# Expert stage of a routed graph layer: the order in which ScalarE and VectorE prepare weights, tokens and results

## The reference, cut to what matters

```
gates = sigmoid(xt @ expert_sel.T);  top 4 experts of each token
scores = relu(einsum('nd,edf->nef', xt, keys)) * gate        # keys   [32, 1024, 512]
out    = einsum('nef,efv->nv', scores, values)               # values [32, 512, 1024]
x = x + out
```

## Time and profile before

| | us |
|---|---|
| median of 3 runs | 999.03 (998.47 to 999.04) |
| profiled execution | 996.85 |
| its span, first to last instruction | 994.9 |
| 29 rounds of the loop over slots, from 558.71 to 953.38 | 13.61 each |
| granted TensorE clock over the span | 0.969 |

### The profile page before, as it was taken

The page is one execution under the profiler, slowest core; times in us unless marked ns, Lnnn a source line. Parts: engine busy times, 40 slices in busy tenths (PEclk is TensorE's granted clock), DMA queues, the critical chain, the costliest instruction groups (busy, mean ns, idle before and its releaser), DMA issues.

```text
span 994.9 us, 14101 instructions
## 1 busy us (share of the span) xinstructions
PE 901.2 (91%) x4447; PEld 739.3 (74%) x4447; DVE 678.9 (68%) x1128; ACT 508.6 (51%) x710; POOL 330.3 (33%) x294
## 2 busy tenths in 40 slices
PE   3889999999999999898954999999999999999993
PEld 3878889989989999445833777777777777777772
DVE  6776676633434544674675688888988888888883
ACT  3343322323323322674220587777777777877772
POOL 0613445544440000895001122343323333223331
PEclk9889999999999999999975999999999999999997
DMA  7433322233334333001662399999999999999951
GB/s 300 156 129 125 115 106 85 85 128 127 128 132 170 127 127 127 1 1 43 253 243 74 132 329 324 347 336 340 343 331 333 336 336 336 323 345 338 343 187 20
DMA packets 40454, 203.01 MB, mean 204 GB/s; under 512 B 12880, under 2 KB 13136, under 8 KB 18400
## 3 DMA queue, kind: packets, MB, share of 16 engines
q1 hardware_dynamic: 25632, 183.51, 50.1%
q0 software_dynamic: 13200, 15.03, 6.2%
q10 hardware_dynamic: 1584, 3.97, 1.0%
HBM read 203.33 MB, written 21.15 MB: 226 GB/s over the span
## 4 chain that ended last, share of the span: by engine, by line
PE 61%; DVE 16%; issue 9%; POOL 6%; ACT 4%; DMA 2%; ACTq 0%; DVEq 0%; POOLq 0%; SPq 0%
PE ps L1074 19%; PE ps L1076 18%; PE ps L1075 18%; POOL pr L375 6%; DVE wl L794 3%; ACT wh_x L618 3%; DVE xgTl L1029 3%; DVE wl_x L794 2%; DVE hTl L1035 2%; PE ps L1104 1%; PE ps L1191 1%; DMA acc<-in_x 1%; DVE etmp L1041 1%; PE ps L1114 1%; DVE ysb L1041 1%
## 5 line engine op out<-in xcount | busy, mean ns | idle before, releaser
L608 ACT ACTIVATE wh<-raw 128x1024 fp32r<-128x1024 f32 x88 | 93.2, 1061 | 251.6 <-PE ps L1076 240.7
L755 DVE TENSOR_TENSOR wl<-raw,wh 128x1024 fp32r<-128x1024 f32 x88 | 109.8, 1252 | 154.8 <-ACT wh L608 154.4
L525 POOL DMA_INDIRECT plane<-code,idx x96 | 100.5, 1047 | 119.4 <-DMA plane<-code,idx 81.4
L1074 PE MATMUL ps<-wh,xgTh 128*128 128x512 f32 x248 | 101.0, 407 | 20.1 <-DVE wl L794 20.1
L1074 PE MATMUL ps<-wh_x,hTh 128*128 128x512 f32 x248 | 105.8, 427 | 0.0
L794 DVE TENSOR_TENSOR wl_x<-raw_x,wh_x 128x1024 fp32r<-128x1024 f32 x64 | 76.7, 1222 | 34.4 <-ACT wh_x L618 34.4
L1076 PE MATMUL ps<-wh,xgTl 128*128 128x512 f32 x248 | 98.0, 395 | 0.0
L1075 PE MATMUL ps<-wl,xgTh 128*128 128x512 f32 x248 | 97.8, 395 | 0.0
L1076 PE MATMUL ps<-wh_x,hTl 128*128 128x512 f32 x248 | 97.7, 394 | 0.0
L1075 PE MATMUL ps<-wl_x,hTh 128*128 128x512 f32 x248 | 97.3, 392 | 0.0
L794 DVE TENSOR_TENSOR wl_x<-raw,wh_x 128x1024 fp32r<-128x1024 f32 x64 | 76.6, 1220 | 29.9 <-ACT wh_x L618 29.9
(11 more groups left out here) (218 smaller groups left out, 2050.7 us busy)
## 6 DMA issues: line engine op xcount, KB each, us to landing
raw<-in_keys SPq DMA_DIRECT2D x34, 1024.0 KB, 10.7
raw_x<-in_values SPq DMA_DIRECT2D x34, 1024.0 KB, 10.7
raw_x<-in_keys SPq DMA_DIRECT2D x30, 1024.0 KB, 11.2
raw<-in_values SPq DMA_DIRECT2D x30, 1024.0 KB, 12.0
raw<-in_w_v SPq DMA_DIRECT2D x8, 1024.0 KB, 4.8
raw<-in_w_q SPq DMA_DIRECT2D x8, 1024.0 KB, 4.8
raw<-in_w_k SPq DMA_DIRECT2D x8, 1024.0 KB, 4.7
raw<-in_w_mq SPq DMA_DIRECT2D x4, 1024.0 KB, 7.8
```

What stands on the lines that cost most here:

```text
L525: nc.gpsimd.indirect_dma_start(plane[m], bass.IndirectOffsetOnAxis(idx[:, g:g + 1].bitcast(U32), 0), code[:, g:g + 1], None, bounds_check= ...
L608: nc.scalar.activation(wh[:, s % SUB], raw[:, c % RAW, 2 * (s % 2):2 * (s % 2) + 2, :], ACT.Copy)\
L755: nc.vector.tensor_tensor(wl[:, s % SUB], raw[:, (s // 2) % RAW, 2 * (s % 2):2 * (s % 2) + 2, :], wh[:, s % SUB].bitcast(F32), ALU.subtrac ...
L1074: nc.tensor.matmul(o, ah, bh_, start=start, stop=False)
```

## The change: what it does

- ScalarE and VectorE take splits 12 to 15, 16 and 17, 18 and 19 in a slot in place of 8 to 15: each follows the sub-chunk that TensorE has just used. Splits 8 to 11 of the first slot come ahead of the loop. Splits 16 to 19 are left out in the last slot.
- The two halves of the transposed tokens are taken by one instruction of 128 x 1024 over two banks, on ScalarE (`x_hi`) and on VectorE (`x_lo`). The eight banks are one tensor now, in the same places.
- y is copied by one ScalarE instruction of 128 x 1024 over two banks (`y_out`), after splits 18 and 19. VectorE's half (`y_first`) goes. One semaphore `s_ye` is left of two.
- GpSimd waits for `s_ye` once. TensorE waits for the whole of y two slots before, ahead of each half.

```diff
-                pool_wait(s_ye0, s + 3)
-                pool_wait(s_ye1, s + 3)
+                pool_wait(s_ye, s + 3)
...
             def x_hi(count, p):
                 act.wait_ge(s_xT, count)
-                for b in range(2):
-                    ins = nc.scalar.activation(xgTh[p][:, 4 * b:4 * b + 4, :], ps[2 + b][:, :].rearrange("p (c t) -> p c t", t=P), ACT.Copy)
-                ins.then_inc(s_xhi, 1)
+                nc.scalar.activation(xgTh[p][:, :, :], x_banks, ACT.Copy).then_inc(s_xhi, 1)
...
-            def y_second(j, p, used):
+            def y_out(j, p, used):
                 act.wait_ge(s_used, used)
                 act.wait_ge(s_scd, 2 * j + p + 1)
-                nc.scalar.activation(ysb[p][:, HALF:D], ps[5 + 2 * p][:, :], ACT.Copy).then_inc(s_ye1, 1)
+                nc.scalar.activation(ysb[p], y_banks[p], ACT.Copy).then_inc(s_ye, 1)
 
             def act_slot(j, p, ahead):
                 k = 8 * p
                 used = SUBS + 8 * p + 16 * j
-                for q in range(8, 10):
+                for q in range(12, 16):
                     split_expert(k + q, j)
                 h_out(used + 8, 2 * j + p + 1)
-                split_expert(k + 10, j)
                 if ahead:
                     x_hi(2 * j + p + 3, p)
-                split_expert(k + 11, j)
+                    for q in range(16, 18):
+                        split_expert(k + q, j)
                 h_hi(2 * j + p + 2, 1 - p)
-                for q in range(12, 14):
-                    split_expert(k + q, j)
-                y_second(j, p, used + 12)
-                for q in range(14, 16):
-                    split_expert(k + q, j)
+                if ahead:
+                    for q in range(18, 20):
+                        split_expert(k + q, j)
+                y_out(j, p, used + 12)
...
             x_hi(2, 1)
+            for k in range(8, 10):
+                split_expert(k, 0)
             h_out(SUBS + 4, 0)
             h_hi(1, 0)
+            for k in range(10, 12):
+                split_expert(k, 0)
...
-            def y_first(j, p, used):
-                dve.wait_ge(s_used, used)
-                dve.wait_ge(s_scd, 2 * j + p + 1)
-                nc.vector.tensor_copy(ysb[p][:, 0:HALF], ps[4 + 2 * p][:, :]).then_inc(s_ye0, 1)
-
             def dve_slot(j, p, ahead):
                 k = 8 * p
-                for q in range(8, 11):
+                for q in range(12, 16):
                     split_expert(k + q, j)
                 if ahead:
                     x_lo(2 * j + p + 3, p)
-                split_expert(k + 11, j)
-                y_first(j, p, SUBS + 10 + 8 * p + 16 * j)
+                    for q in range(16, 18):
+                        split_expert(k + q, j)
                 h_lo(2 * j + p + 2, 1 - p)
-                for q in range(12, 16):
-                    split_expert(k + q, j)
+                if ahead:
+                    for q in range(18, 20):
+                        split_expert(k + q, j)
...
-                pe.wait_ge((s_ye0, s_ye1)[v], 2 * j + p + 1)
+                pe.wait_ge(s_ye, 2 * j + p + 1)
```

More of the change, by code:

```diff
@@ L189, in gps_layer_kernel @@
         wl_x.append(at("wl_x3", [P, 2, HALF], FR, BIV)[:, :, :])
-        ysb = [at("ysb0", [P, D], F32, F1 + 8 * KB), etmp[:, :, :].rearrange("p a b -> p (a b)")]
+        ysb = [at("ysb0", [P, D], F32, F1 + 8 * KB)[:, :], etmp[:, :, :].rearrange("p a b -> p (a b)")]
         call = sb("c_all", [P, sum(w for _, w in CONSTS_AT)], F32)
@@ L214, in gps_layer_kernel @@
         slots = sb("slots", [P, 1], I32)
-        ps = [ctx.enter_context(nc.psum_tensor(f"ps{b}", [P, 512], F32)) for b in range(8)]
+        banks = ctx.enter_context(nc.psum_tensor("ps", [P, 8, 512], F32))
+        ps = [banks[:, b, :] for b in range(8)]
+        x_banks = banks[:, 2:4, :].rearrange("p b (c t) -> p (b c) t", t=P)
+        y_banks = [banks[:, 4 + 2 * p:6 + 2 * p, :].rearrange("p b n -> p (b n)") for p in range(2)]
         s_x = [sem(f"s_x{t}") for t in range(NT)]
@@ L269, in gps_layer_kernel @@
         s_hlo = sem("s_hlo")
-        s_ye0, s_ye1 = sem("s_ye0"), sem("s_ye1")
+        s_ye = sem("s_ye")
         s_sc = sem("s_sc")
@@ L549, in pool_slot @@
                 pool_wait(s_pch, count + 1)
-                pool_wait(s_ye0, s + 3)
-                pool_wait(s_ye1, s + 3)
-                nc.gpsimd.indirect_dma_start(out, bass.IndirectOffsetOnAxis(pcol[:, :].bitcast(U32), 0), ysb[p][:, :], None,
+                pool_wait(s_ye, s + 3)
+                nc.gpsimd.indirect_dma_start(out, bass.IndirectOffsetOnAxis(pcol[:, :].bitcast(U32), 0), ysb[p], None,
                                              bounds_check=N - 1, oob_is_err=False, compute_op=ALU.add).then_inc(s_sc, 16)
@@ L711, in act_slot @@
                 used = SUBS + 8 * p + 16 * j
-                for q in range(8, 10):
+                for q in range(12, 16):
                     split_expert(k + q, j)
                 h_out(used + 8, 2 * j + p + 1)
-                split_expert(k + 10, j)
                 if ahead:
                     x_hi(2 * j + p + 3, p)
-                split_expert(k + 11, j)
+                    for q in range(16, 18):
+                        split_expert(k + q, j)
                 h_hi(2 * j + p + 2, 1 - p)
-                for q in range(12, 14):
-                    split_expert(k + q, j)
-                y_second(j, p, used + 12)
-                for q in range(14, 16):
-                    split_expert(k + q, j)
+                if ahead:
+                    for q in range(18, 20):
+                        split_expert(k + q, j)
+                y_out(j, p, used + 12)
             act.wait_ge(s_tab, 1)
             last = act.value_load(slots[0:1, 0:1], min_val=PAIRS_MIN - 1, max_val=PAIRS_MAX - 1)
-            act.sem_inc(s_ye1, 2)
+            act.sem_inc(s_ye, 2)
             x_hi(1, 0)
             x_hi(2, 1)
+            for k in range(8, 10):
+                split_expert(k, 0)
             h_out(SUBS + 4, 0)
             h_hi(1, 0)
+            for k in range(10, 12):
+                split_expert(k, 0)
             with act.Fori(0, last) as j:
@@ L736, in _ @@
             act_slot(last, 0, False)
-            y_second(last, 1, SUBS + 16 + 16 * last)
+            y_out(last, 1, SUBS + 16 + 16 * last)
         @block.vector
@@ L1027, in x_lo @@
                 dve.wait_ge(s_xhi, count)
[L1028 to L1031, removed]
+                nc.vector.tensor_tensor(xgTl[p][:, :, :], x_banks, xgTh[p][:, :, :].bitcast(F32), ALU.subtract).then_inc(s_xlo, 1)
             def h_lo(count, p):
@@ L1048, in dve_slot @@
                     x_lo(2 * j + p + 3, p)
-                split_expert(k + 11, j)
-                y_first(j, p, SUBS + 10 + 8 * p + 16 * j)
+                    for q in range(16, 18):
+                        split_expert(k + q, j)
                 h_lo(2 * j + p + 2, 1 - p)
-                for q in range(12, 16):
-                    split_expert(k + q, j)
+                if ahead:
+                    for q in range(18, 20):
+                        split_expert(k + q, j)
             dve.wait_ge(s_tab, 1)
             last = dve.value_load(slots[0:1, 0:1], min_val=PAIRS_MIN - 1, max_val=PAIRS_MAX - 1)
-            dve.sem_inc(s_ye0, 2)
             for k in range(6, 8):
@@ L1066, in _ @@
             dve_slot(last, 0, False)
-            y_first(last, 1, SUBS + 14 + 16 * last)
         @block.tensor
```

## The result

The changed kernel takes 983.5 us (median of 4 runs, 981.07 to 984.27) beside 998.84 us (998.47 to 999.04) for the kernel before: a ratio of 0.984 (0.9825 to 0.9861), 15.3 us faster. I had forecast 992.3, a gain of 6.7, and 983.5 is the very end of my range. In the two profiled executions the times are 996.85 and 983.91 and the spans 994.9 and 982.1, a gain of 12.8; the other 2.4 us are scatter between executions.

A forecast was written before the change was run, and what follows sets the result against it. GpSimd's round of adds, at least 13.05 us, was taken to set TensorE's pace, with TensorE and the loads near their end too. Terms -1.8, -3.8 and -1.1 made -6.7: 999.0 to 992.3 us, range 983.5 to 1002.5.

The forecast's parts named there:

- Splits ahead: VectorE's splits 12 to 15 come earlier, so TensorE's wait of 1.1 us a round goes, up to 33 us in all.
- The new pace: GpSimd's round of adds: at least 13.05 us plus 0.40 lost beside VectorE's splits, 13.45 in place of 13.61.
- the adds at their limit before: In the kernel before, GpSimd's adds set TensorE's pace: at least 13.05 us a round, taking 13.61.
- The 0.9 us between the tokens' landing and `x_T`: Cover at TensorE's x_T: if TensorE runs further ahead of GpSimd, it waits there and takes the adds' pace.
- my signs: Wrong if x_T shows no wait for tokens, adds take much over 11.4 us to land, or ScalarE waits for loads.
- The loads: Weight loads: the last part of a load arrives at about 13.8 us a round; 12 us of cover shrink to 8.
- Rival B: GpSimd meets no split, pace 13.05, then the loads bind; 981 to 988 us, chance 0.18.
- taking y off VectorE gives GpSimd nothing: On GpSimd beside VectorE: only splits, with two SBUF inputs, block it, so moving y's copy gains nothing.
- the first rounds: Start of the loop: the add of slot 4 is issued some 1.8 us earlier, -1.8 (0 to -3).
- the 24 rounds to slot 28: Rounds of adds up to slot 28 at 13.45 us in place of 13.61: -3.8 us.
- the end: Last slots: no 1.1 us TensorE stall ahead of slot 30's y, y copied 0.4 later: -1.1 (-2 to 0).

The follow-up runs named there:

- before_loads34: The kernel before with three of the four parts of each expert weight chunk loaded in the loop; 998.3 us, ratio 1.0004.
- banks_only: The kernel before with only the wide two-bank copies of tokens and y, splits in the old order; 993.68 us, ratio 0.9952.
- few_gathers: The changed kernel with the gathers' index bound set to 0, so hardly a token row moves, adds and loads kept; 967.25 us, ratio 0.967.

## Why the prediction was wrong

*Splits ahead: right, in full.* TensorE's 1.1 us a round went at once. The first 16 rounds are 1.04 shorter.

*The new pace: the step that failed.* I wrote: "It is 13.05 plus what GpSimd loses beside VectorE's splits" and took 13.45. The 13.05 was a landing of 11.4, taken as fixed, and 1.65. But the earlier trace rows had the issue at 2.54 us and the earlier trace rows the same instruction at 1.61 where VectorE is quiet, and a landing is counted from the start of the issue. About 1.0 us of the 11.4 was the rest of a split, so the landing proper is 10.4 and the floor 12.05. In the first part of the changed kernel the adds do land in 10.4 and 10.8 us, 0.6 to 1.0 less, and their issues are some 0.8 shorter (1.75 and 1.79 on the mean in 640 to 930). I had counted VectorE's blocking ahead of the issue (0.55), and not inside it. Measured with 1.2 us added, a round of adds is at most 12.4 to 12.8 in the changed kernel, 0.7 to 1.0 under the 13.45 of the forecast. Nor were the adds at their limit before, as I had them: `before_loads34` frees the adds by 4 us a round and the pace stays at 13.60. The 0.9 us between the tokens' landing and `x_T` was real slack, for GpSimd followed TensorE at 13.6 and had more in reserve. Of my signs, one of being wrong came (ScalarE waits for loads), and the wait for the gather at `x_T`, which was to replace the wait for `wl`, is 1.7 us of TensorE's time in 640 to 930.

*The loads: right in kind and size, wrong in place.* The 13.8 us a round that I read from the growth of their landing is what the second part runs at, 13.79. Other growths agree: that in the first part gives 13.7, and in `banks_only`, at 13.45 a round, loads of keys land in 5.8 us in 560 to 600 and in 15.5 in 900 to 940, 0.4 more a round, which makes 13.8 too. Rival B had this: no blocking, then the loads bind, 981 to 988. It has the mechanism that came, with two differences. The first part ran at TensorE's 12.57, not at 13.05, and the cover was more than my 12 to 13 us, since the first loads land in 8.7: it was used up after 16 rounds. And then the whole rest ran at the loads' pace and gave 2.4 us back.

*What blocks GpSimd, and what caps the loads.* The issue is longer by just the rest of a split with two inputs in SBUF, in all five cases above. The Trainium skill (SBUF — State Buffer, "Who interferes with whom", practical consequences) names a GpSimd instruction that reads SBUF as what such a VectorE instruction blocks; the trace agrees, for `pcol` and for the issue of an indirect DMA. I drew from it that taking y off VectorE gives GpSimd nothing. That nearly stands: in `banks_only`, with y off VectorE and the splits in their old places, the issues take 2.42 and 2.37 us, for 2.54 and 2.62. The new place of the splits gives more, 1.75 and 1.79. For the loads, the 94% in the earlier trace rows went with a cap of 13.8 us a round, but the share does not make it: `few_gathers` has 99.4% and 12.65 a round. The Trainium skill's row on uneven engines (DMA: Bandwidth & Descriptors, "Latency and other measured facts") would be in keeping with a cap below a full mean; no row here shows single engines, so it is not shown.

*Terms.* My terms run from add to add. The adds of slots 4, 16, 28 and 31 in the changed kernel, then that of slot 28 before:

```profile
621.12 1.61 POOL L555 DMA_INDIRECT out_dram<-ysb,pcol  x1 [2.23 <-issue]
...
772.23 1.61 POOL L555 DMA_INDIRECT out_dram<-ysb,pcol  x1 [1.47 <-ACT ysb L707]
...
939.59 1.61 POOL L555 DMA_INDIRECT out_dram<-ysb,pcol  x1 [3.28 <-ACT ysb L707]
...
969.67 1.58 POOL L555 DMA_INDIRECT out_dram<-etmp,pcol  x1 [1.05 <-issue]
```

```profile
951.16 2.54 POOL L553 DMA_INDIRECT out_dram<-ysb,pcol  x1 [1.17 <-issue]
```

With 624.55, 787.86 and 982.46 for slots 4, 16 and 31 before: the first rounds gave -3.4 for -1.8 forecast; the 24 rounds to slot 28 gave -8.1 for -3.8, a pace of 13.27 for 13.45, made of 12 rounds at 12.59 (-12.2) and 12 at 13.95 (+4.1), neither of which I had; the end gave -1.2 for -1.1. Sum of the spans -6.7 against -12.8, and -15.3 between the medians. Of the 6.1 between -6.7 and -12.8 4.3 are the failed pace, and 1.6 the first rounds, where the adds held TensorE no more than later.

*The end: right in number, not in its parts.* ScalarE still waited for loads there, 1.3 us for values and 1.1 for keys after 939, with `y_out` and `h_out` behind those splits, and I had no such wait; what it cost was not taken apart, so the match is in part luck. Counted from the last `x_T` the end is 1.2 longer than before, because the add of slot 28 no longer comes 2.2 us ahead of that `x_T`.

*What stays open.* Why 9% of the bytes, in gathers and adds, keep loads of 84% of the DMA engines' time from landing for 24 us, and why the loads stop at 94% and 327 GB/s when the first part moved 359 (their landing grew all the while) and `few_gathers` reached 99.4%. The runs show that the rows' traffic does it and that either half of it is too little. How it does it was not tried: the profile gives the mean of the 16 engines, and no run here moved rows from one engine to another.

## What to carry to other kernels

When a row is taken as a floor, look for the same instruction elsewhere in the trace, on a quiet stretch: if it is shorter there, the floor holds another engine's work, and the change may move it. To learn which of several engines near their limit sets the pace, free one of them and see whether the pace moves; a small slack between two engines that run at the same pace says nothing about who leads. And a gain in a loop that prefetches lasts only as long as the cover: compare the new pace with the pace at which transfers land, and multiply each by its own rounds.

## What was not expected of the hardware

- An indirect DMA's issue on GpSimd took 1.49 us and the rest of the VectorE split (two SBUF inputs, 1.22 us) that was running at its start: 1.79, 2.30, 2.03, 2.54 and 2.62 in the rows above. The splits behind the first did not hold it longer, and an issue that started 0.03 us behind a split's start was not held, at 1.61.
- Loads of 1 MB landed in 24 us beside gathers and adds with 11% of the DMA engines' time, in 6.3 without the adds' rows, in 10.6 without the gathers', and in 4.8 without either, with the DMA engines over 90% busy in each.
- One instruction over two banks of PSUM, 128 x 1024, took 1.006 us on ScalarE where one bank took 0.598, and 1.225 on VectorE where one took 0.683: 0.19 and 0.14 saved for each pair.
